# One core, a hybrid of eight layers: the order of two attention stages laid by a static scheduler, products in pieces

## The reference

```python
scores = jnp.einsum('bqhd,bkhd->bhqk', q, k) * scale
probs = jax.nn.softmax(scores, axis=-1)
attn = jnp.einsum('bhqk,bkhd->bqhd', probs, v).reshape(B, T, D_MODEL)
...
x = _layer_norm(src + attn, ln1_g, ln1_b)
keys = (x @ router_w + router_b)[..., 0]
expert_idx = jnp.remainder(jnp.floor(keys).astype(jnp.int32), N_EXPERTS)
for e in range(N_EXPERTS):
    h = jax.nn.relu(x @ W1[e] + b1[e])
    y = h @ W2[e] + b2[e]
    ff_out = ff_out + jnp.where((expert_idx == e)[..., None], y, 0.0)
return _layer_norm(x + ff_out, ln2_g, ln2_b)
```

## Time and profile before

| what | value |
|---|---|
| device time, median of 2 runs | 4732.12 us (4727.67 to 4736.58) |
| span of the profiled execution | 4609.9 us; 122.2 us less than that median |
| busy in the span | PE 82%, DVE 70%, ACT 61%, POOL 25% |
| alibi, first to last scores | 88.66 to 587.52 us |
| stream, first max, first scores, last scores, end | 2074.40, 2118.95, 4466.00, 4594.50 us |

### The profile page before, as it was taken

The page is one execution under the profiler, slowest core; times in us unless marked ns, Lnnn a source line. Parts: engine busy times, 40 slices in busy tenths (PEclk is TensorE's granted clock), DMA queues, the critical chain, the costliest instruction groups (busy, mean ns, idle before and its releaser), DMA issues.

```text
span 4609.9 us, 92060 instructions
## 1 busy us (share of the span) xinstructions
PE 3765.8 (82%) x36864; PEld 1564.1 (34%) x36864; DVE 3223.7 (70%) x4668; ACT 2810.4 (61%) x5452; POOL 1146.2 (25%) x1376
## 2 busy tenths in 40 slices
PE   4888976677677687838999898989999999989872
PEld 1334443234243355522223232323222222333232
DVE  4777734664654577519987877777979999888921
ACT  2676832431422455415877778787988988768761
POOL 3212001011001023231133443433121122352413
PEclk7999988888888778757999999999999999999996
DMA  2222101110100000011132313131111111313213
GB/s 83 62 54 62 20 17 24 23 24 1 23 2 0 8 1 1 1 55 20 51 85 52 98 46 95 42 95 42 47 46 20 48 50 23 106 47 95 62 44 97
DMA packets 141118, 204.34 MB, mean 44 GB/s; under 512 B 51906, under 2 KB 88770, under 8 KB 140436
## 3 DMA queue, kind: packets, MB, share of 16 engines
q1 hardware_dynamic: 123924, 137.97, 12.2%
q0 software_dynamic: 16768, 60.49, 4.3%
HBM read 123.34 MB, written 64.68 MB: 41 GB/s over the span
## 4 chain that ended last, share of the span: by engine, by line
PE 55%; DVE 21%; issue 6%; ACT 6%; POOL 4%; DMA 4%; SPq 3%; POOLq 0%; DVEq 0%; ACTq 0%
PE ps L1170 12%; DVE stream_max_pieces L1370 8%; PE ps L1143 8%; PE ps L1155 5%; PE ps L598 3%; PE ps L1948 3%; PE ps L557 2%; PE ps L1256 2%; PE ps L240 2%; PE ps L1264 2%; PE ps L2696 2%; DVE mamba_conv_sum L2991 1%; SPq L874 1%; PE ps L578 1%; ACT stream_probs L1282 1%
## 5 line engine op out<-in xcount | busy, mean ns | idle before, releaser
L1370 DVE TENSOR_REDUCE stream_max_pieces<-ps 128x2 f32<-128x1024 f32 x1536 | 1793.1, 1214 | 312.6 <-PE ps L1155 301.0
L1282 ACT ACTIVATE stream_probs<-ps 128x512 f32<-128x512 f32 x3072 | 1653.7, 600 | 333.3 <-PE ps L1143 310.7
L1170 PE MATMUL ps<-stream_probs,stream_v 128*16 128x256 f32 x12288 | 982.3, 392 | 33.4 <-issue 32.2
L1155 PE MATMUL ps<-stream_k_stack,stream_q_stack 48*128 48x512 bf16 x3072 | 656.6, 394 | 109.9 <-DVE stream_max_pieces L1370 77.6
L1143 PE MATMUL ps<-stream_q_stack,stream_k_stack 51*128 51x512 bf16 x3072 | 676.1, 394 | 27.0 <-ACT stream_probs L1282 10.3
L737 DVE TENSOR_REDUCE alibi_max_pieces<-ps 128x2 f32<-128x1024 f32 (+3 forms) x384 | 355.4, 952 | 142.8 <-PE ps L582 133.3
L678 ACT ACTIVATE alibi_probs<-ps 128x512 f32<-128x512 f32 (+3 forms) x768 | 333.8, 492 | 176.8 <-PE ps L563 142.5
L1170 PEld LDWEIGHTS ps<-stream_probs,stream_v 128*16 128x16 f32 x12288 | 203.5, 94 | 663.1 <-issue 362.6
L1143 PEld LDWEIGHTS ps<-stream_q_stack,stream_k_stack 51*128 51x128 bf16 x3072 | 181.6, 93 | 669.2 <-ACT stream_probs L1282 500.3
L362 POOL CAST stream_negmax_parts<-stream_negmax_t 128x32 bf16<-128x32 f32 x96 | 23.0, 240 | 1134.4 <-DVE stream_negmax_t L1359 1088.7
L1155 PEld LDWEIGHTS ps<-stream_k_stack,stream_q_stack 48*128 48x128 bf16 x3072 | 157.9, 95 | 160.8 <-DVE stream_max_pieces L1370 121.8
(11 more groups left out here) (448 smaller groups left out, 5410.0 us busy)
## 6 DMA issues: line engine op xcount, KB each, us to landing
stream_q_terms_dram<-stream_q_parts SPq DMA_DIRECT2D x72, 256.0 KB
stream_k_terms_dram<-stream_k_parts SPq DMA_DIRECT2D x72, 256.0 KB
stream_q_stack<-stream_q_terms_dram SPq DMA_DIRECT2D x96, 192.0 KB, 4.5
stream_k_stack<-stream_k_terms_dram SPq DMA_DIRECT2D x96, 192.0 KB, 4.5
delta_v_shifted<-delta_v_padded SPq DMA_DIRECT2D x64, 158.0 KB, 3.5
alibi_q_terms_dram<-alibi_q_parts SPq DMA_DIRECT2D x24, 256.0 KB
alibi_k_terms_dram<-alibi_k_parts SPq DMA_DIRECT2D x24, 256.0 KB
alibi_q_stack<-alibi_q_terms_dram SPq DMA_DIRECT2D x32, 192.0 KB
```

What stands on the lines that cost most here:

```text
L1155: ins = e.matmul(c.ps[:, mbank(key) + r, :], qs[R, buf, pair, qt * P:(qt + 1) * P], ks[R, buf, pair, kh * 512:kh * 512 + 512], start=True, ...
L1170: ins = e.matmul(c.ps[32 * j:32 * j + 16, 7, Q], v[:, b % 2, kt, GH * g + j, :], pr[:, (u + j // 2) % RP, j % 2, Q], start=(n == 0 and k = ...
L1282: e.activation(pr[:, u % RP, r, :], c.ps[:, ebank(key), :], ACT.Exp, scale=SCALE).then_inc(s_ed, 1)
L1370: e.tensor_reduce(mx[:, j % 2, kh, 4 * pair + qt % 4, :], c.ps[:, mbank(key):mbank(key) + 2, :], AXX, ALU.max).then_inc(s_md, 1)
```

## The change

It replaces the fixed offsets of both stages by a scheduler (class Flow) that lays the list when the program is built. It keeps a clock of its own for PE, ACT, DVE and POOL and a table of planned prices, and picks the next item of PE's among: the next max (up to 56 units ahead of the scores), the next scores (once the half's rows are planned to be there: 1 us of POOL and 7.5 us behind its turn), half of the values of a pair, and the next piece of a side product. Among those that can begin within 30 ns of the earliest, the lowest rank is taken, and a form that PE is already in lowers the rank. Negate, turn, copy, load and out are items of their own, set when their inputs are there.

Side products are cut in pieces that may stand apart: q and k in two of 256 columns, transposes in twos, y in four pieces, w2 in pieces of three matmuls. The due places of the moe work are others; scale stands in six parts, scatter and gather in pairs. On the very last batch the second normalisation on DVE stays.

w2 goes to the E ring: its bias is one more matmul with a contraction of one row (a row of ones by the bias, L1598 now), 88 in all, and ACT copies the result (L1685 now) into a new buffer ys, which the gather writes too. DVE's addition of the bias is gone. The tile of v is 9 columns wide instead of 16, and the clearing of v on POOL at the start of both stages is gone. Form changes on PE in stream: 3306 places. The lead of max over scores runs from 19 to 55 units in stream.

```diff
+class Flow(Plan):
+    MOST, STAY = 56, {"pair": 0.6, "values": 0.6, "side": 4}
+    MODE_NS = 95
+    LAND_NS, ROWS_NS, LATE = 250, 7500, 8
...
+            options = self.choices()
...
+            now = min(max(begin, self.pe) for begin, _, _ in options)
+            _, _, run = min((o for o in options if max(o[0], self.pe) <= now + 30), key=lambda o: o[1])
+            run()
...
+        def option(begin, rank, mode, run):
+            options.append((begin, rank - (self.STAY[mode] if mode == self.mode else 0), run))
+
+        if not self.m_open and self.top < min(self.units, self.loads * self.step, self.next + self.MOST):
+            option(self.m_done[-2], 0 if ahead <= 0 else 1, "pair", self.maximum)
...
+                option(max(self.e_done[-3], self.e_done[-2], self.rows_at[half]), 0.5, "pair", self.scores)
+        if self.paired + 1 < self.next:
+            option(self.values_ready(), 2 if self.next - self.paired < RP - 1 else -1, "values", self.values)
...
+        return 0.42 * cols + 60 * diag, 71 + 0.833 * cols
...
+        return 0.42 * cols + 60 * diag, 63 + 2.084 * cols
...
+    def on_pe(self, begin, mode, ns):
+        begin = max(begin, self.pe)
+        if mode != self.mode:
+            begin, self.mode = begin + self.MODE_NS, mode
+        self.pe = begin + ns
...
+        self.pool = max(self.pool, self.dve) + 1000
+        self.rows_at[j] = self.pool + self.ROWS_NS
...
-        yield 15, ("scale", n, 0)
+        for k in range(6):
+            yield 15 + 3 * k, ("scale", n, 0, k)
...
-        yield 53, ("scatter", n)
+        for k in range(4):
+            yield 55 + 2 * k, ("scatter", n, k)
...
-            yield 88 + 4 * j, ("h", n, j)
+            yield 88 + 6 * j, ("h", n, j)
...
-            yield min(97 + 8 * i, 131), ("w2", n, i)
+            yield min(97 + 12 * i, 151), ("w2", n, i)
...
-        yield 138, ("gather", n)
+        for k in range(4):
+            yield 158 + k, ("gather", n, k)
...
-    plan = Stream(CHAIN, 40)
+    plan = Stream(CHAIN)
...
-    v = sb("v", [P, 2, TPB, NH, 16])
+    v = sb("v", [P, 2, TPB, NH, HD + 1])
...
-                ins = e.matmul(c.ps[32 * j:32 * j + 16, 7, Q], v[:, b % 2, kt, GH * g + j, :], pr[:, (u + j // 2) % RP, j % 2, Q],
+                ins = e.matmul(c.ps[32 * j:32 * j + HD + 1, 7, Q], v[:, b % 2, kt, GH * g + j, :], pr[:, (u + j // 2) % RP, j % 2, Q],
...
+                for j, f in steps[W2 * k:W2 * k + W2]:
+                    to = c.ps[:, ebank(key), (j % 2) * P:(j % 2 + 1) * P]
+                    if f < NF:
+                        ins = e.matmul(to, hid[:, j % NHB, f, :], wb[:, j % NWB, NF * P + f * D:NF * P + (f + 1) * D], start=(f == 0), stop=False)
+                    else:
+                        ins = e.matmul(to, ones[:, :], wb[0:1, j % NWB, EB2:EB2 + D], start=False, stop=True)
...
+                e.activation(ys[:, 2 * k:2 * k + m, :].rearrange("p t d -> p (t d)"), src[:, 0:m * P], ACT.Copy).then_inc(s_ed, 1)
...
-                e.tensor_tensor(xs[:, j:j + m, :], c.ps[:, mbank(key), 0:m * P].rearrange("p (t d) -> p t d", t=m), wb[:, j % NWB:j % NWB + m, EB2:EB2 + D], ALU.add).then_inc(s_md, 1)
...
-        e.memset(v[:, :, :, :, :], 0.0).then_inc(s_zero, 1)
-        e.wait_ge(s_zero, 1)
```

More of the change, by code:

```diff
@@ L660, in chunks @@
+        for key in plan.rows:
+            kind, n = key[:2]
+            if kind == "scores":
+                scores(n)
+            elif kind == "max":
+                max_scores(n)
+            elif kind == "values":
+                values(n, key[2])
+            elif kind == "part":
+                part(n, key[2])
     def chunks(i):
@@ L758, in vector @@
+        for key in plan.rows:
+            kind, n = key[:2]
+            if kind == "max":
+                maximum(n)
+            elif kind == "negate":
+                negate(n)
+            elif kind == "turn":
+                turn(n)
+            elif kind == "out":
+                finish(key)
             elif kind == "norm":
@@ L807, in gpsimd @@
         e.wait_ge(s_set, NSET)
-        for kind, n in plan.rows:
-            if kind == "unit":
-                if n + plan.lead - 1 in plan.ends:
-                    max_split(plan.ends[n + plan.lead - 1])
+        for key in plan.rows:
+            kind, n = key[:2]
+            if kind == "turn":
+                max_split(n)
             elif kind == "norm":
@@ L989, in stream, with pool_cost @@
+    def pool_cost(self, key):
+        kind = key[0]
+        if kind == "split":
+            return 1040 if key[3] % 2 == (self.kind(key[1]) == "rms") else 2140
+        if kind == "scale":
+            return (1930, 3200, 3200, 2360, 2360, 2360)[key[3]]
+        return {"norm": 1900, "xn": 6400, "out_bias": 2360, "scatter": 1950, "gather": 1950, "weights": 970}.get(kind, 0)
 def stream(core, name):
@@ L1075, in stream, with moe_before @@
     s_var = [S(f"moe_variances_ready{k}") for k in range(2)]
-    NSET = 7
+    NSET = 8
     nth = lambda n: plan.count("moe", n)
     uses = [len(range(i, ET, NWB)) for i in range(NWB)]
+    def moe_before(n):
+        return max(i for i in range(n) if plan.kind(i) == "moe")
     def x1_of(n):
@@ L1190, in unit, with part @@
                 ins.then_inc(s_mf, 1)
[L1192 to L1202 removed]
+        def part(key, k):
             kind, n = key[:2]
[L1204 to L1205 removed]
+            if kind == "out":
+                out(key, k)
@@ L1267, in chunks @@
+                if W2 * k + W2 >= len(steps):
+                    ins.then_inc(s_ef, 1)
+        for key in plan.rows:
+            kind, n = key[:2]
+            if kind == "scores":
+                scores(n)
+            elif kind == "max":
+                max_scores(n)
+            elif kind == "values":
+                values(n, key[2])
+            elif kind == "part":
+                part(n, key[2])
     def chunks(i):
@@ L1398, in vector @@
             kind, n = key[:2]
-            if kind == "unit":
-                unit(n)
+            if kind == "max":
+                maximum(n)
+            elif kind == "negate":
+                negate(n)
+            elif kind == "turn":
+                turn(n)
+            elif kind == "out":
+                finish(key)
             elif kind == "norm":
```

866 lines of the change are left out of this document (539 added, 327 removed).

## The result

The changed kernel takes 4610.4 us (4606.2 to 4614.5) against 4732.1: a ratio of 0.975, 95% interval 0.971 to 0.978. Measured again on another chip in one job, it took 4606.0 against 4717.0 (ratio 0.976, 0.974 to 0.978). So 111 to 122 us are gone; 144 had been forecast.

A forecast was written before the change was run, and what follows sets the result against it. The prediction took PE to bound some stretches and DVE others, with PE waiting under a fixed order. Gains of 93 (stream), 12 (head), 12 (tail) and 27 (alibi) made 144, so 4732 became 4588 us, range 4480 to 4740.

The forecast's parts named there:

- rival D: Whole kernel: PE's waits stay the same in sum, form changes save only 12 us, time 4730 us; chance 0.12.
- The time outside the span: Whole kernel: 122 us between the profiled span of 4609.9 and the timed 4732.1 us, kept as they are.
- The order of stream: Stream, first to last scores: maxes that PE skips and makes up for cut 2347 to 2254 us, a gain of 93.
- The 97% for PE's share: Stream: PE's 2186 us of work taken at 97% busy, between 96.8% and 97.8% of two stretches, giving 2254 us.
- form changes count by their number: Stream, PE: 3426 changes of form fall to 3306, 120 at 0.1 us each, saving 12 us.
- The bias matmuls: Stream, PE: 88 added w2 bias matmuls at 0.25 us cost 22 us; 18 us more if one row changes mode.
- The head: Head of stream: 27 maxes before the first scores instead of 40, a gain of 12 us, bounds 0 and 15.
- The tail: End of stream: POOL's scale of batch 10 goes behind the last batch's scatter, a gain of 12 us, bounds 0 and 14.
- Alibi: First stage: all of it comes to its last stretch's 94.0% PE share, 472 us, a gain of 27, bounds 0 and 40.
- A (balance): Whole kernel: full balance, PE at 98% and never slowed by its clock, time 4500 us; chance 0.14.
- B: Stream: scores wait for late rows in 30 of 96 halves, 342 us, time 4930 us; chance 0.11.
- C: Stream: rows late for one half in each of 7 moe batches, 80 us in all, time 4668 us; chance 0.17.

The follow-up runs named there:

- e1: The kernel before, unchanged, profiled a second time and timed against itself: 4717.4 against 4717.0 us, ratio 1.000.
- e3: The kernel before with scatter and gather of the moe stages listed in pairs instead of eights: 4706.7 against 4722.8 us, ratio 0.996.
- e4: The changed kernel with scatter and gather of the moe stages in eights again: 4635.1 us, ratio 0.980 to the kernel before.
- e8: The changed kernel with maxima at most 40 units ahead of their scores instead of 56: 4616.5 us, ratio 0.978 to the kernel before.
- e2: The changed kernel, unchanged, measured again in one job with the kernel before: 4606.0 us, ratio 0.976.
- e7: The changed kernel with the scheduler indifferent to PE's current form and a form change planned at 0 ns: 4727.4 us, ratio 1.002 to the kernel before.
- e11: The changed kernel with the w2 bias matmul contracted over 128 rows instead of one: 4578.0 against 4720.7 us for the kernel before, ratio 0.969.
- e12: The changed kernel with w2 in the maxima's banks again and its bias added on DVE: 4608.6 us, ratio 0.976 to the kernel before.
- e6: The changed kernel meant to place every side product in one go; the edit moved no instruction: 4615.5 us, ratio 0.976 to the kernel before.

## Why the prediction was right, point by point

Direction, size and the listed orders were right, and the size was in part luck: the parts miss in both directions (27 forecast for alibi, 12 for a tail that lost 7, 22 for bias matmuls that took 55), and the largest part rests on a profile that was not typical. Of the signs that it named, two came: the first scores 15 us sooner, and the last scatter ahead of batch 10's scale. The others did not: stream's sum is 2364, not 2254 and even above the 2330 that it gave as a sign of rival D, the stretch with key and rank has PE at 83% and a clock of 0.83 (batch 2), and alibi has PE at 89%, as before.

**The time outside the span: wrong.** The prediction kept 122 us as lying around the span. It is 2 us. The step was to take one execution for all; two timed runs 2.6% above a span should have been a question. It spoiled every share read as "now": in e1 the second stretch of batch 2 takes 62.42 us, where the earlier trace rows shows 49.14.

**The order of stream: 93 forecast, 85 measured.** The size was right with a wrong baseline: from the earlier trace rows, 2347.05, the changed kernel's 2363.98 would be a loss of 17. From e1 the same steps would have given 2211 + 22 - 12 = 2221, at 97% 2290: 153 us in stream and 204 in all, for 111 measured. That the two errors nearly cancel is luck. Of the 85, 16 to 20 are scatter and gather in parts (e3, e4), which the prediction named as an aid for POOL without pricing it, and took for real pairs ("behind 2 scatters instead of 8"), which they are not on POOL. The 97% for PE's share was reached in the stretches with w2 (99.8%), and missed where key, rank and scatter stand (83%): in sum 93.1%. The stretches from which the time was to come, those that DVE holds with key and rank, gave none: the second ones take 63 us more in sum, with the gather and second norm that moved there; the time came in the third and fourth. That the gain comes from maxes left out and made up for is argued: the order shows it, e8 shows that it needs no long lead, but no run forbids it. A rival that stays open is the late exponentials, 106 us in e1 and 70 in e2. That form changes count by their number, 12 us, fell with e7.

**The bias matmuls: 22 forecast, about 55.** Summed from the start of each group of w2 or bias to the start of the next group on PE, w2 with its bias takes 139 us in e2 and 84 in e1. The sentence from the Trainium skill, page "TensorEngine Tiling (Array Packing)", section "Key Properties", that a changed tiling mode drains TensorE, had been set beside the sum with 18 us. By e11 a matmul of one row between those of 128 does cost that much more, and 27 us; that leaves 28 for 88 more matmuls, for which 22 was forecast. Whether TensorE drains there no trace shows. This was the mis-sized term that could have been mended at once. ACT's room for the copies was misread too: the w2 stretch has 56.89 - 43.33 = 13.6 us free, not 16; e12, without them, is no faster.

**The head: 12 forecast, 15 measured.** 27 maxes took 29.66 us; the step holds.

**The tail: 12 forecast, 7 lost.** The scatter of the last batch does stand ahead of batch 10's scale, and the part up to its landing is shorter: from last scores 65.5 us in e1, 59.9 in e2. It isn't 12 shorter because, as the prediction had said, the last batch's own rank is next: POOL idles 4.4 us for it before the weight gather below. What came behind is longer, 63.3 then 75.7 us. In the chain of the changed kernel (start, us, what):

```profile
4505.01 1.68 POOL stream_expert_weights L1940
...
4510.72 1.00 POOL stream_slots_dram L1931
...
4519.69 2.23 DMA stream_slots_dram<-stream_x,stream_positions_int
...
4568.83 3.87 DMA stream_expert_out_dram<-stream_expert_out
...
4596.11 1.22 DVE x L1439
```

From the scatter's landing at 4521.9 on there is no attention to hide behind: eleven tiles of h and w2, each with its bias matmul and, by pairs, a copy on ACT. The prediction looked at the scatter and not at the exposed chain that its own bias term stood in. The runs show it: from the landing to the store of the experts' output it is 34.9 us in e1, 47.1 in e2, 40.0 with the bias over 128 rows (e11) and 37.8 with it on DVE (e12).

**Alibi: 27 forecast, 6 to 9 measured.** The step was "all of it comes to the 94% of its last stretch". That stretch has no next batch to load; the others wait for store and load of k_stack, which the prediction had no row for.

**Rivals.** A (balance) came true in the w2 stretches alone. B and C failed by the 5.3 us above. D, that it doesn't do what it says, failed by its time (4730), but is right in one thing: no product was ever split up (e6), and the count of changes isn't what pays (e7).

## What to carry to other kernels

Price a small matmul by the form of its neighbours, not by its size: here a one-row bias cost 0.41 us and its 128-row twin 0.22, and took back 28 us of 4606. A greedy planner's result belongs to its numbers: four edits of one or two of them moved this kernel by 10, 97, 106 and 121 us, and higher prices, meant to be truer, made it slower; 64 us of that fell in alibi, where the waits that grew (loads of the next step) had no price at all; so measure the order, not the model. And before a profile is read, hold its span against the timed runs; if they differ by more than the kernel's scatter, profile again.

## What had not been expected of the hardware

Two profiles of one program differ by 104 us, and about as much lies beside the rows of eight indirect DMAs: 27 exponentials started 1.9 to 7.7 us later than their own matmul and their free engine allowed (e1), 106 us in sum, and not one in the first profile. A one-row fp32 matmul of 128 columns between 128-row ones takes 0.41 us, start to start, for 0.22 with 128 rows, and the w2 matmuls beside it 1.09 for 0.89; the granted clock was 1.00 in the stretches with w2.
